# A bias row fetched for each sequence, spread by GpSimd and added by VectorE, in place of a one-hot product on TensorE

## What is computed

```
attn    = tanh(x @ W1 + b1)                     # 512 -> 128
scores  = attn @ v                              # one number for each position
p       = softmax(where(mask, scores, -1e30))   # mask: l <= j, l >= j or l != j, by the sequence's type
x       = x + (p @ x) / count(mask)             # first layer
x       = x + x @ W[cat] + b[cat]               # second layer, cat: the sequence's category, 0 to 63
```

## Time and profile before

| What | Value |
|---|---|
| Median of 3 runs | 347.25 us (347.15 to 347.75) |
| The profiled execution: its time | 348.24 us |
| The profiled execution: its span | 346.5 us |
| Mean granted TensorE clock | 0.98 of full speed |
| TensorE busy | 328.6 us, 95% of the span |
| ScalarE busy | 257.0 us |
| VectorE busy | 245.0 us |
| GpSimd busy | 4.7 us |

### The profile page before, as it was taken

How to read it: one execution, slowest core, us unless ns; L and a number is a source line. 1 busy time by engine, 2 the same in 40 slices (tenths; PEclk the granted TensorE clock), 3 DMA queues, 4 the chain that set the end, 5 groups by cost and what they waited for, 6 DMA issues and landing times.

```text
span 346.5 us, 4558 instructions
## 1 busy us (share of the span) xinstructions
PE 328.6 (95%) x1352; PEld 239.4 (69%) x1352; DVE 245.0 (71%) x225; ACT 257.0 (74%) x373; POOL 4.7 (1%) x19
## 2 busy tenths in 40 slices
PE   7473999999999999999999999999999999999996
PEld 5252777777767777777776777777777777777773
DVE  1559679594949769494968859494977949495810
ACT  2568387795968777795978779696977779596832
POOL 5000000000000000000000000000000000000000
PEclk9969699999999999999999999999999999999999
DMA  6999768999899888989898898989889899863113
GB/s 162 354 424 421 283 257 285 348 307 377 271 303 338 298 341 289 373 291 341 293 308 331 289 347 301 383 291 332 309 274 363 283 357 308 310 210 129 62 61 121
DMA packets 21641, 101.55 MB, mean 293 GB/s; under 512 B 2706, under 2 KB 2706, under 8 KB 11634
## 3 DMA queue, kind: packets, MB, share of 16 engines
q1 hardware_dynamic: 21458, 100.94, 80.3%
q0 software_dynamic: 160, 0.33, 0.9%
HBM read 84.48 MB, written 16.78 MB: 292 GB/s over the span
## 4 chain that ended last, share of the span: by engine, by line
PE 89%; DMA 4%; DVE 3%; SPq 2%; issue 1%; ACT 0%; DVEq 0%
PE ps_y L489 17%; PE ps_y L490 16%; PE ps_y L491 16%; PE ps_y L500 16%; PE ps_pre L456 13%; PE ps_y L502 4%; DMA w_raw<-in_L_cond_W 4%; PE ps_scores L464 4%; PE ps_pT L477 2%; DVE w_lo L359 1%; PE ps_scores L466 1%; DVE xT_lo L346 1%; DVE w_raw L335 1%; SPq L176 0%; SPq L153 0%
## 5 line engine op out<-in xcount | busy, mean ns | idle before, releaser
L359 DVE TENSOR_TENSOR w_lo<-w_raw,w_hi 128x2048 fp32r<-128x2048 f32 x63 | 143.9, 2284 | 0.1
L251 ACT ACTIVATE w_hi<-w_raw 128x2048 fp32r<-128x2048 f32 x63 | 121.8, 1934 | 4.3 <-DVE w_raw L335 4.3
L489 PE MATMUL ps_y<-w_hi,xT_hi 128*128 128x512 f32 x256 | 104.1, 407 | 5.2 <-DVE w_lo L352 4.9
L490 PE MATMUL ps_y<-w_lo,xT_hi 128*128 128x512 f32 x256 | 101.2, 395 | 0.0
L491 PE MATMUL ps_y<-w_hi,xT_lo 128*128 128x512 f32 x256 | 100.4, 392 | 0.0
L500 PE MATMUL ps_y<-z_sb,mix 128*128 128x512 f32 x128 | 65.2, 591 | 0.0
L489 PEld LDWEIGHTS ps_y<-w_hi,xT_hi 128*128 128x128 f32 x256 | 48.8, 191 | 19.3 <-DVE w_lo L352 5.3
L364 DVE TENSOR_REDUCE neg_max<-ps_scores 128x4 f32<-128x512 f32 x16 | 11.1, 692 | 69.7 <-PE ps_scores L466 69.7
L491 PEld LDWEIGHTS ps_y<-w_hi,xT_lo 128*128 128x128 f32 x256 | 48.5, 190 | 11.1
L490 PEld LDWEIGHTS ps_y<-w_lo,xT_hi 128*128 128x128 f32 x256 | 48.6, 190 | 9.2
L502 PE MATMUL ps_y<-b_both,one_hot 128*128 128x512 f32 x64 | 50.8, 794 | 0.0
(11 more groups left out here) (58 smaller groups left out, 174.2 us busy)
## 6 DMA issues: line engine op xcount, KB each, us to landing
w_raw<-in_L_cond_W SPq DMA_DIRECT2D x63, 1024.0 KB, 7.4
out<-out_sb SPq DMA_DIRECT2D x64, 256.0 KB, 5.0
x_raw<-in_x SPq DMA_DIRECT2D x15, 1024.0 KB, 9.2
x_raw<-in_x SPq DMA_DIRECT2D x2, 512.0 KB, 6.1
w_raw<-in_L_cond_W SPq DMA_DIRECT2D x2, 512.0 KB, 9.8
w_raw<-in_L_cond_W SPq DMA_DIRECT2D x1, 256.0 KB, 7.1
b_raw<-in_L_cond_b POOLq DMA_DIRECT2D x2, 128.0 KB, 8.3
type_all<-in_itok_B POOLq DMA_DIRECT2D x1, 32.0 KB, 6.8
```

The costliest lines, as they stand in the source:

```text
L251: nc.scalar.activation(w_hi[k % NH][:], w_raw[k % NW][:], ACT.Copy).then_inc(w_hi_ready, 1)
L359: nc.vector.tensor_tensor(w_lo[k % NL][:], w_raw[k % NW][:], w_hi[k % NH][:].bitcast(F32), ALU.subtract).then_inc(w_lo_ready, 1)
L489: nc.tensor.matmul(y[:], xT_hi[q][:, c, xs], w_hi[k % NH][:, c, :], start=(c == 0), stop=False)
L490: nc.tensor.matmul(y[:], xT_hi[q][:, c, xs], w_lo[k % NL][:, c, :], start=False, stop=False)
```

## The change

The one-hot product is gone, and all that fed it: the loads of the bias and of the categories to all partitions, the rounding, and VectorE's five instructions. In its place:

- SP gets `load_bias(k)`: it reads the category again and fetches the one bias row of 2 KB into partition 0 of `b_row` (3 buffers). Three are issued after the first matrices; later ones stand in each step t between the store of t-3 and the load of matrix t+7, for sequence t+2, behind a wait for the broadcast of t-1.
- GpSimd (POOL) does one `partition_broadcast` for each sequence, from `b_row` to all partitions of `b_all` (3 buffers), once the row has landed and the addition of three sequences earlier is done.
- VectorE does the copy out: `add_bias(k-3)`, the sum of the PSUM bank and `b_all` into `out_sb`, at the head of pass k. ScalarE's `copy_out` is gone.

```
-            pool.dma_start(cat_all[:], ...).then_inc(cat_all_in, 16)
-            pool.dma_start(b_raw[0:C, :], bias).then_inc(b_low_in, 16)
-            pool.dma_start(b_raw[C:P, :], bias).then_inc(b_high_in, 16)
+            for k in range(B):
+                pool.wait_ge(b_row_in[k % NB], 16 * (k // NB + 1))
+                if k >= NB:
+                    pool.wait_ge(out_ready, k - NB + 1)
+                nc.gpsimd.partition_broadcast(b_all[k % NB][:], b_row[k % NB][:], channels=P).then_inc(b_all_ready, 1)
...
+            def load_bias(k):
+                cat = sp.value_load(cat_row[0:1, k:k + 1], min_val=0, max_val=C - 1)
+                if k >= NB:
+                    sp.wait_ge(b_all_ready, k - NB + 1)
+                sp.dma_start(b_row[k % NB][:], bias[bass.ds(cat, 1)]).then_inc(b_row_in[k % NB], 16)
...
                 if t >= 3:
                     store(t - 3)
+                if t >= 1 and t + 2 < B:
+                    load_bias(t + 2)
...
-            def copy_out(k):
-                act.wait_ge(pz_done, k + 1)
-                if k >= NO:
-                    act.wait_ge(out_stored[k % NO], 16 * (k // NO))
-                nc.scalar.activation(out_sb[k % NO][:], ps_y[k % NY][:], ACT.Copy).then_inc(out_ready, 1)
...
+            def add_bias(k):
+                dve.wait_ge(pz_done, k + 1)
+                dve.wait_ge(b_all_ready, k + 1)
+                if k >= NO:
+                    dve.wait_ge(out_stored[k % NO], 16 * (k // NO))
+                nc.vector.tensor_tensor(out_sb[k % NO][:], ps_y[k % NY][:], b_all[k % NB][:], ALU.add)\
+                    .then_inc(out_ready, 1)
...
-            for k in range(B):
+            for k in range(B + 3):
                 g, b = k // G, k % G
                 if k == 0:
                     max_group(0)
+                if k >= 3:
+                    add_bias(k - 3)
...
-                nc.tensor.matmul(y[:], mix[g % 2][:, b, :], z_sb[k % NZ][:], start=False, stop=False,
-                                 skip_group_check=True)
-                nc.tensor.matmul(y[:], one_hot[:, k:k + 1].to_broadcast([P, P]), b_both[:],
-                                 start=False, stop=True, skip_group_check=True).then_inc(pz_done, 1)
+                nc.tensor.matmul(y[:], mix[g % 2][:, b, :], z_sb[k % NZ][:], start=False, stop=True,
+                                 skip_group_check=True).then_inc(pz_done, 1)
```

More of the change, by code:

```diff
@@ L36, in program @@
     HALF = DC // 2
-    NX, NW, NH, NL, NZ, NO, NY = 2, 5, 4, 3, 3, 4, 5
+    NX, NW, NH, NL, NZ, NO, NY, NB = 2, 5, 4, 3, 3, 4, 5, 3
     ctx = ExitStack()
@@ L74, in program @@
         warm = sb("warm", [P, 256], BF16)
-        b_raw = sb("b_raw", [P, D], F32)
-        b_hi = sb("b_hi", [P, D], F32R)
-        b_both = sb("b_both", [P, D], F32R)
+        b_row = [sb(f"b_row{i}", [1, D], F32) for i in range(NB)]
+        b_all = [sb(f"b_all{i}", [P, D], F32) for i in range(NB)]
         cat_row = sb("cat_row", [1, B], I32)
-        cat_all = sb("cat_all", [P, B], I32)
         type_all = sb("type_all", [P, B], I32)
@@ L84, in program @@
         type_row = sb("type_row", [1, B], I32)
[L85 to L89, removed]
+        row_i = sb("row_i", [P, 2], I32)
+        row_f = sb("row_f", [P, 2], F32)
         seen = sb("seen", [P, B], F32)
@@ L101, in program @@
         types_in = sem("types_in")
-        cat_all_in = sem("cat_all_in")
-        b_low_in = sem("b_low_in")
-        b_high_in = sem("b_high_in")
+        b_row_in = [sem(f"b_row_in{i}") for i in range(NB)]
         x0_in = [sem(f"x0_in{h}") for h in range(2)]
@@ L117, in program @@
         w1_lo_ready = sem("w1_lo_ready")
-        b_hi_ready = sem("b_hi_ready")
-        bias_ready = sem("bias_ready")
+        b_all_ready = sem("b_all_ready")
         wi_ready = sem("wi_ready")
@@ L184, in _ @@
             load_w(4)
+            for k in range(NB):
+                load_bias(k)
             for t in range(-2, B + 3):
@@ L296, in _ @@
             split_w_hi(1)
-            act.wait_ge(b_low_in, 16)
-            act.wait_ge(b_high_in, 16)
-            nc.scalar.activation(b_hi[:], b_raw[:], ACT.Copy).then_inc(b_hi_ready, 1)
             split_w_hi(2)
-            for k in range(B + 3):
+            for k in range(B + 1):
                 g, b = k // G, k % G
@@ L305, in _ @@
                     copy_z(k - 1)
-                if k >= 3:
-                    copy_out(k - 3)
                 if b == 0 and g + 1 < GROUPS:
@@ L385, in _ @@
             split_x0_lo(1)
-            dve.wait_ge(consts_ready, 8)
+            dve.wait_ge(consts_ready, 7)
             add_identity_0(0)
@@ L404, in _ @@
                 .then_inc(setup_step, 1)
[L405 to L410, removed]
+            dve.wait_ge(setup_step, 5)
             nc.vector.scalar_tensor_tensor(seen[:], is_postfix[:], row_f[:, 1:2], is_prefix[:],
                                            ALU.mult, ALU.add).then_inc(seen_ready, 1)
[L413 to L417, removed]
             dve.wait_ge(seen_ready, 1)
             add_identity(3)
-            for k in range(B):
+            for k in range(B + 3):
                 g, b = k // G, k % G
@@ L513, in _ @@
             pe.wait_ge(kinds_ready, 1)
-            pe.wait_ge(consts_ready, 8)
+            pe.wait_ge(consts_ready, 7)
             kinds = [load_kind(i) for i in range(G)]
@@ L531, in _ @@
                         kinds += [load_kind(G * (g + 1) + 3)]
-                if k == 2:
-                    pe.wait_ge(bias_ready, 3)
                 if k >= 2:
```

## The result

| | Median of the runs | Ratio to before (95% interval) |
|---|---|---|
| before | 347.5 us (4 runs) | |
| changed | 337.06 us (336.02 to 337.56, 4 runs) | 0.969 (0.966 to 0.972) |

The changed kernel is 10.4 us faster. The forecast was 333.0 us, with 329.5 to 339 as the forecast's own range. The profiled execution took 337.50 us with a span of 334.6 us, against 348.24 and 346.5.

A forecast was written before the change was run, and what follows sets the result against it. TensorE bounds the kernel before; VectorE was to end just over it. From 348.24 us, -14.7 (products) - 1.8 (ramp) + 2.4 (VectorE) = 334.1, median stated as 333.0 us; own range 329.5 to 339, 8 in 10: 329.5 to 350.

The forecast's parts named there:

- c: What VectorE loses to one GpSimd broadcast: estimated at 0.5 us, possible from 0 to 1.17.
- VectorE's 19.0 us: VectorE's work in a group, 17.5 + 1.5 us, just over TensorE's: +0.17 us a group, 2.4 us over 14 periods.
- TensorE's 14.7 us: Saving on TensorE from dropping 64 bias products at 0.23 us each; a group goes from 19.75 to 18.83 us.
- VectorE's additions: Four 128 x 512 bias additions a group on VectorE, 0.61 us each, up to 0.69 possible; 2.44 us a group.
- 17.5 + 3c: VectorE's time a group: 15.05 us plus 2.44 for additions, plus three exposed broadcasts; pass 3's has cover.
- GpSimd's broadcast: 64 broadcasts of 512 words on GpSimd, 0.13 + 0.65 = 0.78 us each; its own time was to cost nothing.
- rival (b): VectorE and GpSimd exclude each other for the whole broadcast: 349 us at c = 0.78, 371 at 1.17; chance 0.20.
- margin of 0.56 us of xT_lo: Without friction, xT_lo ends 10.72 us after the maximum's start and `hidden`, which needs it, starts at 11.28.
- The ramp: Start of the kernel: VectorE's setup and DMA loads leave the chain, 1.8 us gained, 0 to 2.5 possible.
- DMA relief: In the ramp, 256 KB of bias and 32 KB of categories leave full DMA queues: 0.8 us, of which 0.5 taken.
- rival (c): The DMA feed gives out: a matrix late now and then costs 5 to 10 us, 336 to 341 us; chance 0.05.

The follow-up runs named there:

- e9: The kernel before with only TensorE's one-hot bias product left out, so the bias is missing from the output: 333.00 us, ratio 0.958.
- e8: The changed kernel broadcasting only the first 256 of 512 words, into buffers zeroed once: 332.84 us, one run.
- e4: The changed kernel with four bias buffers and each broadcast released by the last VectorE instruction ahead of the bias addition: 335.95 us, ratio 0.968.
- e2: The changed kernel with every broadcast done twice, the first into a tile that nobody reads: 348.97 us, ratio 1.004.
- e7: The changed kernel with six bias buffers, a one-column iota last in GpSimd's list and e10's earlier broadcast release: 330.93 us, ratio 0.952.
- e10: The changed kernel with four bias buffers and broadcasts released one VectorE instruction sooner than in e4, no iota at the end: 332.98 us, ratio 0.958.
- e5: The kernel before with a single broadcast added at the end of GpSimd's list, into a tile nobody reads: 348.08 us, ratio 1.001.
- e3: The changed kernel with each broadcast replaced by a GpSimd memset of the same tile, so the bias is left out: 330.63 us, ratio 0.950.
- e6: The changed kernel with six bias buffers, the last twelve broadcasts released earlier, and a one-column iota last in GpSimd's list: 335.87 us, ratio 0.964.

## Why the prediction was right, and where it was short

The time came out 4.1 us above the forecast and inside its range, and c was taken at nearly its size. But the mechanism that turned c into time was not the one of the sum. The forecast let VectorE's 19.0 us outgrow TensorE's 18.83. The step that failed is that comparison of sums: VectorE's sum bound in no group, and the loss came from a single c ahead of xT_lo, through a margin that the prediction had worked out without friction. That the one way gives 0.17 us a group and the other 0.30 is luck.

- **TensorE's 14.7 us**: right. e9 alone gives 14.5 from median to median (347.51 to 333.00).
- **VectorE's additions**: 0.68 us recorded and 0.60 apart, as taken (0.61). VectorE's group was forecast at 17.5 + 3c; with c = 0.47 that makes 18.9, and the window has 18.84.
- **GpSimd's broadcast**: 0.78 forecast from a line through two other instructions, 0.80 measured. That is partly luck: 0.55 us for 256 words (e8) and 0.80 for 512 make 1.0 ns a word and 0.3 us beside it, where the forecast had 1.26 ns and 0.13 us.
- **c = 0.5**: 0.47 measured, and it grows with the words, as the prediction said: e8 shows it. The cover that it took off its 0.65 isn't there; the price of a word was too high instead. c stands in three records a group, as in the formula, with the fourth under the maximum, but only the one ahead of xT_lo costs time. The rival (b), exclusion for the whole instruction, would have cost 0.80 and did not come. The Trainium skill, "SBUF — State Buffer", section "Who interferes with whom", is borne out on which pairs exclude each other (w_lo with a broadcast, but not with a memset, nor the addition with its PSUM input). On the second to issue being blocked until the first is through, the runs decide otherwise for the broadcast: VectorE is held 0.47 of its 0.80 us. For VectorE's own instructions it holds: GpSimd's read waits to the end of w_lo.
- **The group**: 19.0 forecast, 19.08 measured, with a floor of 18.83 forecast and 18.78 measured. The distance from the floor is 0.30 rather than 0.17, which makes 1.8 us in 14 groups; the lower floor gives 0.7 back, so the groups account for 1.1 us of the miss. Of the 0.30, 0.25 lie at `hidden` in every group, where it waits for xT_lo; the other 0.01 to 0.07 are spread over its products and the pass behind it, and no run here shows from what. The step that was short: the margin of 0.56 us of xT_lo was worked out without c, and up to the start of `hidden` instead of the moment at which its first weights must be loaded. Measured, xT_lo ends at 10.70 us without a delay (10.72 forecast), and 10.93 still costs nothing (e8), so at least 0.23 is there, not much more: at 11.09 (e4) 0.17 is lost, and at 11.17, with one c, 0.25. VectorE's sum needs a higher price before it binds, as in e2.
- **The ramp**: 1.8 us forecast and 0.2 for a product there, 1.0 measured. The identity of matrix 3 was to come at 25 us and came at 26.82. The removed instructions did go, but the step put two new costs at nothing. GpSimd's selects came at 13.66 us, for which e7 against e10 gives some 2 us. And the first three broadcasts fell on the chain between 23 and 27.5 us, where is_prefix, seen and the identity of matrix 3 took 0.80, 0.55 and 1.09 us, against 0.25, 0.28 and 0.69. On the other side I undersold the DMA relief, 0.5 in the sum: in e7 VectorE has the third matrix at 19.52 us instead of 22.17, and in e5, where the same loads are only issued 10 us later, at 20.5.
- **Outside the span**: 1.73 to 1.84 us in all runs of the kernel before, but 1.7 to 3.0 from one run to another of the faster kernels (2.0 to 2.5 in e9, which has no broadcast). I took 1.74 for all. What it is stays open; it is some 0.5 us of the miss from median to median.
- **SP and DMA**, rival (c): nothing. No instruction of the steady state waits for a DMA, and matrices land in 7.4 us at the median as before.

## What to carry to other kernels

When work goes to an engine with spare time, count its sum, but also the one instruction that the bound engine waits for, and carry every added cost into that margin, up to the moment at which the waiting engine must load its weights. Where a GpSimd instruction reads SBUF, try releasing it while VectorE is busy with an instruction of two SBUF inputs whose successor has at most one: in e10 it waits its turn there and delays nobody. And where GpSimd uses select or iota at the head of its list and a broadcast at the end, try an iota behind it; that was worth some 2 us here.

## What the runs showed of the hardware

- A GpSimd partition_broadcast takes 0.80 us for 512 words and 0.55 for 256. Its read and a VectorE instruction with two SBUF inputs exclude each other, 0.9 ns a word on VectorE's side; a blocked broadcast is recorded with 2.7 to 2.9 us, most of it waiting. The Trainium skill, "Perfetto Trace Analysis", section "GPSIMD Engine Instruction", has the record begin where the first core issues its read; the trace agrees: 163.72 lies before w_lo's end at 165.76, and the record runs to 166.42.
- Also short instructions of VectorE pay: a tensor_scalar over 64 elements with one SBUF tensor and a per-partition scalar was 0.80 us beside a broadcast, against 0.25.
- What stands last in GpSimd's list bears on its first select: with a broadcast last it comes at 13.0 to 13.7 us in all seven such kernels, with an iota or a memset last it comes at 2.9 to 3.3 (the kernel before, e9, e3, e6, e7). That it is the code left by the execution before is my reading; no run here sets it apart from something that is fixed for the whole kernel when it is loaded, which the first execution after another kernel would tell. The wait is 10.1 to 10.8 us ahead of the first select and 7.0 to 7.2 ahead of the late iota. The Trainium skill, "GPSIMD Engine Reference", section "Instruction dispatch", gives approximately 6 us for the first call to freshly loaded code; these waits are longer.
- TensorE loses time at a product whose weights become ready only when it is about to start, since the load then isn't covered: 0.25 us at `hidden`, where xT_lo ends 0.9 us after the start of pz, and none in e8 and e10, where it ends earlier. 0.31 us from that product to the next, for 0.23, is the part that shows in the products behind it.
